# A fused attention and mixture-of-experts kernel: w2 of all experts resident and read by register, w1 loaded by DMA for each row tile, a ring of seven row tiles

## What is computed

```python
# h: 2048 rows of 128 after the second norm; w1, w3: (8, 128, 512); w2: (8, 512, 128)
router_logits = einsum('bsh,he->bse', x, gate)
routing_weights, selected = top_k(router_logits, 2)
routing_weights = softmax(routing_weights)
g = einsum('bsh,ehi->ebsi', x, experts_w1)
u = einsum('bsh,ehi->ebsi', x, experts_w3)
hid = silu(g) * u
eo = einsum('ebsi,eih->ebsh', hid, experts_w2)
out = einsum('ebsh,bse->bsh', eo, tok_w)     # only the 2 chosen experts have a weight
```

## Time and profile before

| | |
|---|---|
| median of 3 runs | 331.8 us (330.05 to 332.74) |
| span of the profiled execution, first to last instruction | 336.7 us |
| its mean granted TensorE clock | 0.923 |
| PE busy, weight loads busy | 279.1 us (83%), 203.3 us (60%) |
| DVE, ACT, POOL busy | 217.2, 183.2, 160.2 us |

### The profile page before, as it was taken

How to read it: one execution, slowest core, us unless ns; L and a number is a source line. 1 busy time by engine, 2 the same in 40 slices (tenths; PEclk the granted TensorE clock), 3 DMA queues, 4 the chain that set the end, 5 groups by cost and what they waited for, 6 DMA issues and landing times. The chain is left out here.

```text
span 336.7 us, 7278 instructions
## 1 busy us (share of the span) xinstructions
PE 279.1 (83%) x2264; PEld 203.3 (60%) x2264; DVE 217.2 (65%) x552; ACT 183.2 (54%) x393; POOL 160.2 (48%) x252
## 2 busy tenths in 40 slices
PE   3558799999999898999798498776999999999700
PEld 2134354555554545454343397776999999999700
DVE  4678879788889789999945648562433333333136
ACT  7432476767776575666654364334566666665400
POOL 4050236255756579696958544635333333333400
PEclk9958899999999999999958789959999999999965
DMA  3842231342526262490112333333355544455365
GB/s 95 175 75 65 65 111 43 96 154 60 209 61 197 71 202 78 102 193 11 42 31 72 97 85 112 104 103 110 105 149 142 144 142 143 141 142 137 95 207 174
DMA packets 57254, 38.22 MB, mean 114 GB/s; under 512 B 5240, under 2 KB 52104, under 8 KB 57216
## 3 DMA queue, kind: packets, MB, share of 16 engines
q1 hardware_dynamic: 52880, 31.16, 34.0%
q0 software_dynamic: 2272, 4.69, 4.2%
q10 hardware_dynamic: 2064, 1.91, 2.1%
HBM read 23.58 MB, written 6.75 MB: 90 GB/s over the span
## 5 line engine op out<-in xcount | busy, mean ns | idle before, releaser
L480 ACT ACTIVATE probs<-psB 128x512 f32<-128x512 f32 x128 | 71.2, 594 | 26.6 <-PE psB L1330 25.0
L913 DVE TENSOR_REDUCE negm<-psA 128x4 f32<-128x1024 f32 x64 | 77.6, 1221 | 11.7 <-PE psA L1308 11.1
L1478 PE MATMUL psA<-qs,kd 128*128 128x128 f32 x624 | 79.6, 283 | 6.2 <-ACT qs L562 6.2
L1478 PEld LDWEIGHTS psA<-qs,kd 128*128 128x128 f32 x624 | 76.3, 200 | 6.6 <-ACT qs L562 6.6
L771 POOL DMA_INDIRECT y_d<-ys,qs x39 | 37.7, 967 | 72.1 <-ACT ys L552 68.6
L1173 DVE TENSOR_TENSOR qs<-psA,kd 128x512 f32<-128x512 f32 x39 | 27.0, 692 | 55.4 <-PE psA L1478 33.3
L643 POOL TENSOR_SCALAR_AFFINE_SELECT probs<-probs 128x512 f32<-128x512 f32 x64 | 39.3, 639 | 35.8 <-ACT probs L480 35.6
L1305 PE MATMUL psA<-kd,qs 96*128 96x512 bf16 x128 | 48.2, 400 | 2.0 <-DVE negm L913 1.5
L1330 PE MATMUL psB<-qs,kd 98*128 98x256 bf16 x256 | 46.9, 282 | 0.5 <-ACT probs L480 0.2
L1488 PE MATMUL psB<-kd,qs 128*128 128x128 f32 x312 | 42.5, 280 | 1.0 <-ACT ys L552 0.6
L1350 PE MATMUL psO<-probs,vx 128*32 128x256 f32 x512 | 39.3, 407 | 1.2 <-POOL probs L643 1.2
(11 more groups left out here) (187 smaller groups left out, 331.5 us busy)
## 6 DMA issues: line engine op xcount, KB each, us to landing
kd<-in_L_ffn_experts_w_dram SPq DMA_DIRECT2D x39, 256.0 KB
w_sb<-in_L_ffn_experts_w_dram SPq DMA_DIRECT2D x8, 512.0 KB
kd<-parts SPq DMA_DIRECT2D x96, 32.0 KB
qs<-parts SPq DMA_DIRECT2D x42, 64.0 KB
mod_sb<-mod_d SPq DMA_DIRECT2D x8, 320.0 KB, 5.0
qs<-xs_d SPq DMA_DIRECT2D x39, 65.0 KB
pay<-pay SPq DMA_DIRECT2D x8, 128.0 KB
probs<-y_d SPq DMA_DIRECT2D x3, 256.0 KB, 4.5
```

The source lines that it names most:

```text
L480: nc.scalar.activation(probs[:, kt, n % PRING], psB[:, kt, :].rearrange("p (h q) -> p h q", h=H2), ACT.Exp).then_inc(s["exped"], 1)
L913: nc.vector.tensor_reduce(negm[:, b % 2, :, :, j], psA[:, n % 2].rearrange("p q (h k) -> p q h k", h=H2), AX.X, ALU.max, negate=True).then ...
L1478: last = nc.tensor.matmul(ps[:, k * P:(k + 1) * P], w[:, r, k * P:(k + 1) * P], xsT[:, r], start=True, stop=True)
```

## The change

w2 of all 8 experts is loaded once, in two halves of 1 MB, into two of the three slots of `kd` as soon as attention has done with them (the slots are renumbered by `slot_of` so that these lie together), and `down` picks the expert's block with an address in a PE register, which PE reads from `tile_e` for each tile. w1 is no longer resident: SP loads the expert's 256 KB for each tile into a ring of three, after `up` of three tiles before, in the place in SP's order where `load_w2` stood. DVE's `w1_copy` is gone. `xs` lies in a free slot of `vx` and has seven slots; `gate_act` lies in `parts`; `w1_t` and `w3_t` have SBUF of their own.

```diff
--- before.py
+++ after.py
...
-    XRING = 5
+    XRING = 7
...
-        w1_sb = sb("w1_sb", [P, E, I])
+        w1_t = sb("w1_t", [P, TRING, I])
+        w3_t = sb("w3_t", [P, TRING, I])
...
-        w1_t = moe_buf("kd", TRING, I)
-        w3_t = moe_buf("kd", TRING, I)
-        w2_t = moe_buf("kd", TRING, I)
-        gate_act = moe_buf("kd", TRING, I)
-        hid = moe_buf("qs", TRING, I)
-        xsT = moe_buf("qs", TRING, P)
-        xs = moe_buf("qs", XRING, W)
...
+        slot_of = lambda b: (b + 1) % RING
...
+        w2_sb = kd_words[:, 0:E * I].rearrange("p (e k c) -> p e k c", e=E, c=C)
+        gate_act = part_words.rearrange("p (r i) -> p r i", i=I)
+        hid = qs_words[:, 0:TRING * I].rearrange("p (r i) -> p r i", i=I)
+        xsT = qs_words[:, TRING * I:TRING * (I + P)].rearrange("p (r c) -> p r c", c=P)
+        XS_SLOT = B // 2 % VRING
+        xs = vx_words[:, XS_SLOT, 0:XRING * W].rearrange("p (r c) -> p r c", c=W)
...
+                if step >= B - 1:
+                    load_w2(step - (B - 1))
...
-                for w_sb, w in ((w1_sb, w1), (w3_sb, w3)):
-                    sp.dma_start(w_sb[:, e:e + 2], w[e:e + 2].rearrange("e c i -> c e i")).then_inc(s["moe_w"], 16)
+                sp.dma_start(w3_sb[:, e:e + 2], w3[e:e + 2].rearrange("e c i -> c e i")).then_inc(s["moe_w"], 16)
...
-            def load_w2(n):
+            def load_w2(half):
+
+                sp.wait_ge(s["scoresB"], 2 * NPAIR * (B - 2 + half))
+                lo = half * E // 2
+                sp.dma_start(w2_sb[:, lo:lo + E // 2].rearrange("p e k c -> p (e k) c"),
+                             w2[lo:lo + E // 2].rearrange("e (k p) c -> p (e k) c", p=P)).then_inc(s["w2_in"], 16)
+
+            def load_w1(n):
 
                 if n >= TRING:
-                    sp.wait_ge(s["y_ps"], n - TRING + 1)
+                    sp.wait_ge(s["g_ps"], n - TRING + 1)
                 e = sp.value_load(tile_e[0:1, bass.ds(n, 1)], min_val=0, max_val=E - 1)
-                sp.dma_start(w2_t[:, n % TRING].rearrange("p (k c) -> p k c", c=C),
-                             w2[bass.ds(e, 1)].rearrange("e (k p) c -> p (e k) c", p=P)).then_inc(w2_in[n % TRING], 16)
+                sp.dma_start(w1_t[:, n % TRING], w1[bass.ds(e, 1)].rearrange("e c i -> c (e i)")).then_inc(w1_in[n % TRING], 16)
...
             sp.wait_ge(s["list_ready"], 2)
-            sp.wait_ge(s["scoresB"], 2 * NPAIR * B)
             for n in range(TRING):
-                load_w2(n)
+                load_w1(n)
+            sp.wait_ge(s["pv"], 8 * (B // 2 + 1))
             for done, count in xs_put_by(EB):
                 sp.wait_ge(done, count)
             for n in range(XRING):
...
-                    load_w2(n + TRING)
+                    load_w1(n + TRING)
...
-            def w1_copy(n, r):
-
-                if n >= TRING:
-                    dve.wait_ge(s["g_ps"], n - TRING + 1)
-                e = expert(n)
-                nc.vector.tensor_copy(w1_t[:, r], w1_sb[:, bass.ds(e, 1), :].rearrange("c o i -> c (o i)")).then_inc(s["w1_ready"], 1)
...
-            w1_copy(0, 0)
-            w1_copy(1, 1)
...
             for n in range(NTILE):
                 gate_hidden(n, n % TRING)
-                if n + 2 < NTILE:
-                    if n + 2 == NEARLY:
-                        dve.wait_ge(s["list_ready"], 4)
-                    w1_copy(n + 2, (n + 2) % TRING)
...
+            def expert(n):
+                if n == NEARLY:
+                    pe.wait_ge(s["list_ready"], 4)
+                return pe.value_load(tile_e[0:1, bass.ds(n, 1)], min_val=0, max_val=E - 1)
...
+                pe.wait_ge(w1_in[r], 16 * (m // TRING + 1))
+                for k in range(NC):
+                    last = nc.tensor.matmul(psG[m % 2][:, k * P:(k + 1) * P], w1_t[:, r, k * P:(k + 1) * P], xsT[:, r], start=True, stop=True)
+                last.then_inc(s["g_ps"], 1)
+                pe.wait_ge(s["w3_ready"], m + 1)
+                for k in range(NC):
+                    last = nc.tensor.matmul(psU[m % 2][:, k * P:(k + 1) * P], w3_t[:, r, k * P:(k + 1) * P], xsT[:, r], start=True, stop=True)
+                last.then_inc(s["u_ps"], 1)
+
+            def down(n, r, e):
                 pe.wait_ge(s["hid_ready"], n + 1)
-                pe.wait_ge(w2_in[r], 16 * (n // TRING + 1))
-                if not first(n):
+                if first(n):
+                    pe.wait_ge(s["w2_in"], 32)
+                else:
                     pe.wait_ge(s["y_ready"], n)
                 for k in range(NC):
-                    last = nc.tensor.matmul(psY, hid[:, r, k * P:(k + 1) * P], w2_t[:, r, k * C:(k + 1) * C],
+                    last = nc.tensor.matmul(psY, hid[:, r, k * P:(k + 1) * P], w2_sb[:, bass.ds(e, 1), k].rearrange("p o c -> p (o c)"),
...
                     up(n + 1, (n + 1) % TRING)
+                e = expert(n)
...
-                down(n, n % TRING)
+                down(n, n % TRING, e)
```

More of the change, by code:

```diff
@@ L184, in adaln_attention_moe @@
         wraw = start[:, 6 * C:8 * C].rearrange("p (w c) -> p w c", c=C)
[L187 to L194, removed]
-        w1_t = moe_buf("kd", TRING, I)
-        w3_t = moe_buf("kd", TRING, I)
-        w2_t = moe_buf("kd", TRING, I)
-        gate_act = moe_buf("kd", TRING, I)
-        hid = moe_buf("qs", TRING, I)
-        xsT = moe_buf("qs", TRING, P)
-        xs = moe_buf("qs", XRING, W)
-        assert NC * P == I and all(used_moe[k] <= moe_space[k].shape[1] for k in used_moe)
+        slot_of = lambda b: (b + 1) % RING
+        kd_words = kd[:].rearrange("p r h q t -> p (r h q t)").bitcast(F32)
+        qs_words = qs[:].rearrange("p r q t -> p (r q t)").bitcast(F32)
+        part_words = parts[:].rearrange("p b i k t -> p (b i k t)").bitcast(F32)
+        vx_words = vx[:].rearrange("p r k q h c -> p r (k q h c)")
+        assert slot_of(B - 1) == 2 and slot_of(B - 2) == 1 and slot_of(B - 3) == 0
+        w2_sb = kd_words[:, 0:E * I].rearrange("p (e k c) -> p e k c", e=E, c=C)
[4 more added lines that the diff above has]
+        xs = vx_words[:, XS_SLOT, 0:XRING * W].rearrange("p (r c) -> p r c", c=W)
+        assert NC * P == I and gate_act.shape[1] == TRING and TRING * (I + P) <= 2 * qs_words.shape[1] // 3
+        assert E * I == 2 * kd_words.shape[1] // 3 and XRING * W <= vx_words.shape[2]
         ybuf = probs[:].rearrange("p k a h q -> p (k a h q)")
@@ L235, in adaln_attention_moe @@
         xs_in = [sem(f"xs_in{r}") for r in range(XRING)]
-        w2_in = [sem(f"w2_in{r}") for r in range(TRING)]
+        w1_in = [sem(f"w1_in{r}") for r in range(TRING)]
         xs_put = [sem(f"xs_put{r}") for r in range(PAYRING)]
@@ L453, in move_q_first @@
                     if QP[slot] == part:
-                        act.dma_start(qs[16 * slot:16 * slot + 16, 0], parts[:, 0, 0, part, :]).then_inc(stack_in[0], 16)
+                        act.dma_start(qs[16 * slot:16 * slot + 16, slot_of(0)], parts[:, 0, 0, part, :]).then_inc(stack_in[0], 16)
             def m_copy(b, half):
@@ L464, in m_copy @@
                     act.wait_ge(s["scoresB"], 16 * (b - RING + 1))
-                act.dma_start(qs[SROWS:SROWS + H2, b % RING, 4 * half:4 * half + 4, :],
+                act.dma_start(qs[SROWS:SROWS + H2, slot_of(b), 4 * half:4 * half + 4, :],
                               mT[:, b % 2, half, :]).then_inc(s[f"m_in{half}"], 16)
@@ L1323, in scores_B @@
                 n = NPAIR * b + j
-                r = b % RING
+                r = slot_of(b)
                 if j % 4 == 0 and kt == 0:
@@ L1470, in xs_T @@
                 nc.tensor.transpose(psX, xs[:, n % XRING, 0:C], ident[:]).then_inc(s[done], 1)
+            def expert(n):
+                if n == NEARLY:
+                    pe.wait_ge(s["list_ready"], 4)
+                return pe.value_load(tile_e[0:1, bass.ds(n, 1)], min_val=0, max_val=E - 1)
             def up(m, r):
                 pe.wait_ge(s["xsT_ready"], m + 1)
-                for ps, w, ready, done in ((psG[m % 2], w1_t, "w1_ready", "g_ps"), (psU[m % 2], w3_t, "w3_ready", "u_ps")):
-                    pe.wait_ge(s[ready], m + 1)
-                    for k in range(NC):
-                        last = nc.tensor.matmul(ps[:, k * P:(k + 1) * P], w[:, r, k * P:(k + 1) * P],
-                                                xsT[:, r], start=True, stop=True)
-                    last.then_inc(s[done], 1)
-            def down(n, r):
+                pe.wait_ge(w1_in[r], 16 * (m // TRING + 1))
[7 more added lines that the diff above has]
+            def down(n, r, e):
                 pe.wait_ge(s["hid_ready"], n + 1)
-                pe.wait_ge(w2_in[r], 16 * (n // TRING + 1))
-                if not first(n):
+                if first(n):
+                    pe.wait_ge(s["w2_in"], 32)
+                else:
                     pe.wait_ge(s["y_ready"], n)
                 for k in range(NC):
-                    last = nc.tensor.matmul(psY, hid[:, r, k * P:(k + 1) * P], w2_t[:, r, k * C:(k + 1) * C],
```

(2 more changed lines are left out.)

20 lines of the change are left out of this document (7 added, 13 removed).

## The result

The changed kernel takes 368.2 us (median of 6 runs, 366.85 to 375.95), the kernel before 332.3 us (6 runs, 330.05 to 336.0): a ratio of 1.109 with the interval 1.101 to 1.117. The profiled execution of the changed kernel took 372.3 us, with a span of 370.5 us. Medians are over all runs of a kernel; ratios compare only runs in the chip's faster state, so they can differ from the ratio of the medians by a few thousandths.

The account below looks back on a forecast made before the run. PE, busy 83% of the span, was taken as the bound, with the loop of y, scatter, SP and row load just behind. 20.8 + 3.9 + 3.1 - 0.4 = +27.4 us on 331.8 gave 359 us, range 347 to 372.

Parts of the forecast that it names:

- Part 1: 39 DVE copies of w1 go, 16.8 us of work off the chain: taken as 0, at most 4 us.
- Part 2: w1 loads queue on SP behind a scatter's wait, so PE waits at every third tile: +20.8 us.
- link: Steady loop, y(k) through scatter, row load and w1 load to y(k+3): 10.7 us against 8.37, 9 times.
- The step from y to the row load: From `y_copy` start to issue of the row load waiting for its scatter: 3.97 us, range 3.68 to 4.80.
- Part 3: SP's late-list wait moves two iterations earlier, holding w1 of tile 10: +3.9 us, and +3.1 for low clock.
- Part 4: PE's register load for each tile is covered by `up`: 0, or up to 16 us if uncovered.
- Part 5: Seven row slots remove a 0.4 us stall: -0.4; w2's halves and attention's loads cost nothing.
- The clock rival: PE's clock falls in each of the 9 gaps, 3.1 us each: 387 us, chance 9%.
- The fixed cost of a DMA: w1's landing: 1.6 us to first byte; the skill's about 2 us would add 1.8 us in all.

Follow-up runs that it names:

- the copies given back: Changed kernel with rows loaded five tiles ahead, plus 37 DVE copies of 128 x 512 into a spare buffer, each with a register load: 334.9 us, ratio 1.002.
- the two edits that undo it in different ways: Changed kernel with rows loaded five tiles ahead, not seven: 334.85 us; changed kernel with five w1 slots, w1 issued two tiles earlier: 335.3 us.
- The quarter of the bytes: Changed kernel, each w1 load bringing 128 of 512 columns (64 KB for 256), which `up` uses four times: 354.6 us, ratio 1.068.
- that version: Changed kernel with w1 loads of tiles 10 to 12 issued ahead of SP's wait for the late list: 359.8 us, ratio 1.084.
- the same block: Changed kernel with rows loaded five tiles ahead, plus SP's wait for the late list and puts in iteration 6: 338.1 us, ratio 1.017.

## Why the prediction was right

It said 359 us (347 to 372) and slower; it is 368.2. The mechanism is the one predicted; the sum of +27.4 us is 8.5 short of the measured +35.9. By its steps:

- **Part 1, DVE's copies at 0.** Shown by the copies given back: 1.002 against 1.003. In the changed kernel DVE was up to 4 us ahead in the steps just before the first y (a step at 188.58 that was at 192.36), and that was worth nothing: y(0) came at 198.9 as before (199.2), and at 201.4 DVE was 0.3 us ahead.
- **Part 2, w1 behind the scatter, +20.8 us.** The mechanism is shown by the two edits that undo it in different ways, both within about 1% of before. The size was off. A link takes (339.45 - 244.41) / 8 = 11.88 us, y(9) to y(33), instead of 10.7. In the mean of the eight late loads, y to the row load is 4.42 us (3.6 to 5.8) where 3.97 was set; row load to w1 load is 1.12 as written; the w1 load to the start of `up` is 2.71 where 2.5 was set; `up` to the next y is 3.63 where 3.09 was set. So of the 1.20 us that a link had too little, 0.45 are the scatter's step, 0.21 the landing and 0.54 PE's own time, and the last is the clock's alone: five of the eight take 3.06 to 3.07 us and three take 4.41, 4.57 and 4.69. A full-speed link and a slow one (PE, then ACT's y):

```profile
313.19 1.13 PE L1469 MATMUL psA<-qs,w_t 128*128 128x128 f32 x8 [2.19 <-DMA w_t<-in_L_ffn_experts_w_dram]
316.25 0.37 ACT L559 ACTIVATE ys<-psB,vx 128x128 f32<-128x128 f32 x1 [0.63 <-PE psB L1483]
300.76 1.80 PE L1469 MATMUL psA<-qs,w_t 128*128 128x128 f32 x8 [3.00 <-DMA w_t<-in_L_ffn_experts_w_dram]
305.45 0.37 ACT L559 ACTIVATE ys<-psB,vx 128x128 f32<-128x128 f32 x1 [0.67 <-PE psB L1483]
```

  The count of links was wrong in the other direction: 9 were counted down from `up(38)`, but `load_xs` ends with tile 38, issued at 334.99 in iteration 31, so the last w1 behind a scatter's wait is that of tile 35, and the last that is late is tile 34's. Eight links at 3.51 us, 11.88 - 8.37, are 28.1 us.
- **The step from y to the row load**, again: the prediction took one pair. The mean of the 14 pairs of before, 4.3 us, was at hand and would have given 11.0 us a link; over all 25 pairs of the steady stretch of before it is 4.4, up to 5.41 and not 4.80. The quarter of the bytes, with 3.74 against 4.26, shows that the w1 loads themselves lengthen it.
- **Part 3, the late wait, +3.9 and +3.1.** Without it 8.4 us less, against 7.0, although that version keeps a gap of 4.1 us of its own; without links the same block costs 4.7. The gap before `up(10)` was 6.79 us where 6.8 was written down, and the clock 0.50 behind it, but the slow stretch was short: `up(10)` to y(9) takes 4.57 us (239.84 to 244.41), 1.5 more than at full clock and not 3.1.

  The +3.9 was net of the 3.0 us stall that the profile of before has at this place. That stall, and the one of 3.2 us at 217, hang on an ACT that something unnamed held up (waits of ACT between 190 and 330 us: in total, how many, the longest):

```profile
ACT kd L546 <- remote: 6.3, 2, 3.2
```

  No other profile of this document has such a wait there, not even those of the two kernels that differ from before only in the ring or in the order of the puts. So the two stalls belong, as far as these profiles show, to that one execution, whose span is 4.9 us over the median. Measured against that profile the stretch to y(9) shows +6.3; there the changed kernel has two smaller gaps for w1 before tile 8, of 2.66 and 2.73 us, where I had written 0. That 7.0 and 6.3 lie so close is luck and not insight.
- **Part 4, PE's register at 0.** Shown: next to no idle time in front of `down` in the trace, and taking the register out leaves the time the same within 0.4%.
- **Part 5, the rest, seven slots worth -0.4.** In the versions with seven slots and no links no stall of that sort is left (2.79 us a tile to the end), so the term stands, small as it is. What the ring costs lies in Part 3. In the kernel before the ring alone costs 1.3%, about 4 us: there I had expected no change, and had not asked closely enough about the w2 load that stands behind the same wait.
- **The clock rival, 387 us.** It came true in part. Of the eight links three had a slow stretch behind their gap, as had the gap before `up(10)`; behind the others `up` went at full speed. Each slow stretch cost 1.3 to 1.6 us and not 3.1, so that 28 us became 4.5. This was a rival of its own at 9%, where it ought to have been a term in the sum: a part of the gaps at a price. The Trainium skill, TensorE: Matmul & The Clock Gate, section HAM oscillation — how this bites in real kernels, tells of a loop that is slow behind every wait for a DMA. The trace agrees in part: three links of eight, a mean clock of 0.95.
- **The fixed cost of a DMA.** Landings of 64 KB in 1.9 us and of 256 KB in 2.6 us give 0.7 us for 192 KB and so, as an estimate, some 1.7 us without data (the rows of the two are of 512 B and 2 KB, which this leaves out). The Trainium skill's page DMA: Bandwidth & Descriptors, section Latency and other measured facts, with its about 2 us would be 0.3 above; the 1.6 us of the earlier trace rows was the nearer.

Part of the nearness of 359 is luck: a link was 1.20 us too small, 9.6 us over the eight, and the ninth link, which doesn't exist, gave 2.3 of them back.

What stays open: why the w1 load takes 2.6 us in one pass and 4.0 in the next, which gaps bring the low clock, and what held ACT in the profile of before.

## What to carry to other kernels

A queue that waits in order turns every wait into a wait for all that stands behind it; so for each load that is moved into a slot of such a queue, set the time at which the wait ahead of it ends against the time at which the load is needed, not against its length. w2 could stand behind the scatter of tile k because it had 10 us, w1 in the same slot had 5.3, and a lead of two more tiles, on either side of the wait, was the whole difference between 368 and 335 us. Lengthening a ring moves all its waits as well: ask what other loads stand behind the longest one of them.

## What was new of the hardware

- A scatter of 64 KB is often slower when a w1 load of 256 KB has just gone out. From POOL's issue of a scatter to the row load that waited for it are 3.0 us where no w1 load went out shortly before (281.09 to 284.06, 306.09 to 309.06), and 3.65 to 5.14 us where one went out within 0.7 us before it (298.44 to 302.09, 316.89 to 320.58, 255.46 to 260.18, 327.96 to 332.77, 291.75 to 296.89). It isn't the only reason: one scatter without a w1 load in the 5 us before it took 4.32 (308.88 to 313.20). With w1 loads of 64 KB the longest step from y to the row load falls from 5.78 to 4.16 us.
- The clock after a gap isn't settled by the gap's length: in the changed kernel it was near 0.50 in most of the `up` behind 6.8, 3.5, 3.0 and 2.73 us, and in part behind one of 1.9 us, but another gap of 2.70 us left it at 1.00. The first line is from the changed kernel, the second from the run with the copies given back, where a gap of the same length brought 0.50:

```profile
336.38 1.13 PE L1469 MATMUL psA<-qs,w_t 128*128 128x128 f32 x8 [2.70 <-DMA w_t<-in_L_ffn_experts_w_dram]
235.14 2.05 PE L1482 MATMUL psA<-qs,w_t 128*128 128x128 f32 x8 [2.70 <-DMA w_t<-in_L_ffn_experts_w_dram]
```

  Eight matmuls in 1.13 us against 2.05. In the quarter of the bytes no stretch from y(9) on was slow, with gaps of at most 1.5 us; its gap of 5.5 us before `up(10)` brought the low clock there too.
- A register load on PE's queue, 0.30 + 0.15 us, costs nothing measurable here, where 1.8 us of matmuls are queued ahead of it (1.003 with it, 0.999 without).
